# Graph kernel, sums of attention values: a table of PSUM addresses in place of VectorE additions

## The reference

```python
score = jnp.einsum('ehc,ehc->eh', q[dst], k[src]) / jnp.sqrt(OUT_C)
m = jax.ops.segment_max(score, dst, num_segments=n)
p = jnp.exp(score - m[dst])
denom = jax.ops.segment_sum(p, dst, num_segments=n)
alpha = p / jnp.maximum(denom[dst], 1e-16)
msg = v[src] * alpha[:, :, None]
out = jax.ops.segment_sum(msg, dst, num_segments=n)
```

## Time and profile before

| what | value |
|---|---|
| median of 3 runs | 6645.76 us (6632.06 to 6658.19) |
| profiled execution, first to last instruction | 6640.4 us |
| mean granted TensorE clock of the execution | 0.798 |
| PE, DVE, ACT, POOL busy | 69%, 58%, 33%, 40% |
| `clear_sums`, from the last instruction before to the first behind it | 3732.97 to 3741.61 us |
| `sum_values`, first to last instruction | 3741.6 to 4277.7 us |

### The profile page before, as it was taken

How to read it: one execution, slowest core, us unless ns; L and a number is a source line. 1 busy time by engine, 2 the same in 40 slices (tenths; PEclk the granted TensorE clock), 3 DMA queues, 4 the chain that set the end, 5 groups by cost and what they waited for, 6 DMA issues and landing times. The chain is left out here.

```text
span 6640.4 us, 100472 instructions
## 1 busy us (share of the span) xinstructions
PE 4599.9 (69%) x23624; PEld 3812.1 (57%) x23625; DVE 3837.8 (58%) x9293; ACT 2210.7 (33%) x4021; POOL 2644.9 (40%) x2513
## 2 busy tenths in 40 slices
PE   4455565565555455555555466549999999999997
PEld 2344444444322233333332355449999999999997
DVE  5466666666545566656566888864444466444443
ACT  0132223232212333333334133224444444334432
POOL 0355555555104565555550000014444444334432
PEclk7777777777787667666676676669999999999999
DMA  0333333333114455555552133233434344323332
GB/s 19 113 88 88 90 89 88 89 88 88 46 50 127 138 151 149 149 145 149 145 145 67 52 103 103 83 107 147 148 142 147 143 171 158 117 107 146 133 129 79
DMA packets 543144, 750.30 MB, mean 113 GB/s; under 512 B 57967, under 2 KB 441966, under 8 KB 542734
## 3 DMA queue, kind: packets, MB, share of 16 engines
q1 hardware_dynamic: 461182, 521.35, 23.4%
q0 software_dynamic: 81552, 224.63, 12.3%
HBM read 584.36 MB, written 161.41 MB: 112 GB/s over the span
## 5 line engine op out<-in xcount | busy, mean ns | idle before, releaser
L557 POOL DMA_INDIRECT arena<-table_kv,arena x1664 | 1684.5, 1012 | 1427.2 <-DVE arena L801 434.5
L2190 PE MATMUL ps<-moving,parts 128*128 128x384 f32 (+1 forms) x11662 | 2016.5, 331 | 38.2 <-ACT moving L2252 20.4
L2190 PEld LDWEIGHTS ps<-moving,parts 128*128 128x128 f32 x11662 | 1950.0, 188 | 71.9 <-ACT moving L2252 29.4
L2131 POOL CAST moving<-counts 128x1152 fp32r<-128x1152 uint8 (+1 forms) x420 | 476.7, 1135 | 1544.7 <-DVE counts L2265 935.6
L311 PE MATMUL ps<-by_place,by_lo 128*128 128x392 bf16 x1568 | 659.5, 525 | 438.7 <-issue 197.3
L320 ACT ACTIVATE counted<-ps 128x392 uint8<-128x392 f32 x1568 | 682.1, 506 | 619.7 <-PE ps L311 276.7
L2131 POOL CAST moving<-big 128x1152 fp32r<-128x1152 uint8 (+1 forms) x413 | 468.4, 1134 | 610.2 <-PE ps L2190 610.2
L667 PE MATMUL ps<-arena 128*128 128x137 f32 x1664 | 350.6, 372 | 370.1 <-DVE arena L801 358.5
L311 PEld LDWEIGHTS ps<-by_place,by_lo 128*128 128x128 bf16 x1568 | 190.0, 126 | 679.3 <-issue 433.9
L301 DVE TENSOR_TENSOR slots<-slots,counted 128x196 uint16 x1568 | 406.3, 259 | 289.0 <-issue 218.1
L667 PEld LDWEIGHTS ps<-arena 128*128 128x128 f32 x1664 | 301.2, 261 | 403.4 <-DVE big L764 190.0
(11 more groups left out here) (291 smaller groups left out, 5326.6 us busy)
## 6 DMA issues: line engine op xcount, KB each, us to landing
counts<-adjacency SPq DMA_DIRECT2D x53, 2352.0 KB, 8.5
big<-adjacency SPq DMA_DIRECT2D x52, 2352.0 KB, 8.6
adjacency<-slots SPq DMA_DIRECT2D x784, 98.0 KB
edge_values<-arena SPq DMA_DIRECT2D x208, 256.0 KB
arena<-edge_values SPq DMA_DIRECT2D x208, 256.0 KB, 3.1
arena<-table_kv,arena POOLq DMA_INDIRECT x1664
big<-table_norm SPq DMA_DIRECT2D x60, 192.0 KB, 5.7
big<-adjacency SPq DMA_DIRECT2D x7, 1568.0 KB, 6.5
```

The source lines that it names most:

```text
L557: pool.indirect_dma_start(m.ring4[r][:, k * 2 * D:(k + 1) * 2 * D], None, table, bass.IndirectOffsetOnAxis(m.src[:, j * HALF + k:j * HALF ...
L2131: pool.tensor_copy(to, of).then_inc(by_pool, 1)
L2190: mm = pe.matmul(m.bank(g % 2, n * P), d.parts[SOURCE[u]][:, s + q, t_, :], moving[:, q * n * P:(q + 1) * n * P], start=(s + q == 0 and t_ ...
```

## The change

The sums no longer pass through VectorE. The 49 blocks are 17 trios of three blocks; a trio's sums (3 x 132 = 396 columns) have one of the eight PSUM banks, trio number modulo 8, and all matmuls of a trio add up there. A half begins on TensorE with a register load of five places from a table, a matmul of zeros onto the bank whose trio is done (`closed`), then come the four matmuls at addresses from registers, then a wait until ScalarE has copied that bank to `m.sums` (`evacuated`), and a matmul of zeros with `start=True` that clears the bank. Each of the 208 halves, and 8 more behind them, moves one bank out, whether a trio is done or not; one that moves nothing of use writes behind the sums. ScalarE reads two of the places. GpSimd takes over the copy of the weights. Inputs of the matmuls have four buffers in place of two, the weighing and the comparison are one instruction each, and `clear_sums` is gone. The table is computed by VectorE in a chain of twenty instructions ahead of its copies in `softmax_rows`.

```diff
+def places_of_blocks(dve, m, ct, vec):
+    def then(op):
+        nonlocal count
+        count += 1
+        op.then_inc(vec, 1)
+        dve.wait_ge(vec, count)
...
+    then(dve.tensor_copy(block_f, m.block[0:1, :]))
+    then(dve.tensor_scalar(trio_i, m.block[0:1, :], 43.0, None, ALU.mult))
...
+    then(dve.tensor_tensor_scan(moved[:, 1:EVACS + 1], one, whole, 0.0, ALU.add, ALU.min))
...
+    then(dve.tensor_scalar(places[:, :, HALF], bank_i, 512.0, None, ALU.mult))
 def sum_values(nc, m, ct, edge_values):
...
+        @block.gpsimd
+        def _(pool):
+            def half(j, r):
+                wait(pool, used, j - 3)
+                pool.tensor_copy(msg[r][:, :, D:A1],
+                                 m.weight[:, ds(j * (HALF * H1), HALF * H1)].rearrange("p (k n) -> p k n", n=H1)).then_inc(weights_ready, 1)
...
         @block.tensor
         def _(pe):
+            regs = registers(nc, pe, "va1pe", HALF + 1)
+            def nought(at, opens):
+                return pe.matmul(m.ps[:, at], nothing[:, 0:P], nothing, start=opens, stop=not opens)
             def half(j, r):
-                pe.wait_ge(hit_ready, j + 1)
-                pe.wait_ge(weights_ready, j + 1)
-                pe.wait_ge(weighted, j + 1)
-                wait(pe, added, (j - 3) * HALF)
-                for k in range(HALF):
-                    mm = pe.matmul(summed(r, k), m.hit[:, r % 2, k, :], m.msg[:, r % 2, k, 0:A1], start=True, stop=True)
-                mm.then_inc(used, 1)
+                last = isinstance(j, int) and j >= 2 * TURNS
+                pe.load(regs, ct.tables[0:1, ds(j * PLACE, HALF + 1)])
+                done = ds(pe.snap(regs[HALF], min_val=0, max_val=(BANKS - 1) * 512), TRIO_SUMS)
+                nought(done, False).then_inc(closed, 1)
+                if not last:
+                    at = [pe.snap(x, min_val=0, max_val=most) for x in regs[:HALF]]
+                    pe.wait_ge(hit_ready, j + 1)
+                    pe.wait_ge(weights_ready, j + 1)
+                    pe.wait_ge(weighted, j + 1)
+                    for k in range(HALF):
+                        mm = pe.matmul(m.ps[:, ds(at[k], A1)], hit[r][:, k, :], msg[r][:, k, :], start=False, stop=False)
+                    mm.then_inc(used, 1)
+                pe.wait_ge(evacuated, j + 1)
+                nought(done, True)
...
         @block.scalar
         def _(act):
+            def convert(j, r):
                 act.wait_ge(hot, j + 1)
+                wait(act, used, j - 3)
+                act.activation(hit[r], hit16[:, r].rearrange("p n k -> p k n"), ACT.Copy).then_inc(hit_ready, 1)
+            def evacuate(j):
+                act.load(regs, ct.tables[0:1, ds(j * PLACE + HALF, 2)])
+                of = act.snap(regs[0], min_val=0, max_val=(BANKS - 1) * 512)
+                to = act.snap(regs[1], min_val=0, max_val=TRIOS * TRIO_SUMS)
+                act.wait_ge(closed, j + 1)
+                act.activation(m.sums[:, ds(to, TRIO_SUMS)], m.ps[:, ds(of, TRIO_SUMS)], ACT.Copy).then_inc(evacuated, 1)
...
+                    convert(4 * i + r + 1, (r + 1) % 4)
+                    evacuate(4 * i + r)
...
         @block.vector
         def _(dve):
+            def half(i, j, r):
+                one_hots(j + 1, (r + 1) % 4)
+                dve.wait_ge(read[r], 16 * i + 16)
+                weigh(j, r)
...
         softmax_weights(nc, m)
-        clear_sums(nc, m, BLOCKS * A1)
         sum_values(nc, m, ct, edge_values)
```

More of the change, by code:

```diff
@@ L48 @@
 SC = COLS * H1
+BANKS = 8
+TRIOS = -(-BLOCKS // 3)
+TRIO_SUMS = 3 * A1
+EVACS = 2 * TURNS + 8
+PLACE = 6
 F32 = mybir.dt.float32
@@ L988, in sum_values @@
 def sum_values(nc, m, ct, edge_values):
-    with Phase(nc, "va1", "used added made hot hit_ready weights_ready weighted read0 read1 read2 read3") as (
-            block, used, added, made, hot, hit_ready, weights_ready, weighted, read0, read1, read2, read3):
+    with Phase(nc, "va1", "used made hot hit_ready weights_ready weighted evacuated closed read0 read1 read2 read3") as (
+            block, used, made, hot, hit_ready, weights_ready, weighted, evacuated, closed, read0, read1, read2, read3):
@@ L994, in sum_values @@
         hit16 = m.stage_c[:, COLS // 2:COLS // 2 + 2 * HALF * P].bitcast(BF16).rearrange("p (a n k) -> p a n k", a=4, k=HALF)
+        nothing = m.prod[:, 0:TRIO_SUMS // 2].bitcast(BF16)
+        hit = [m.hit[:, 0], m.hit[:, 1], m.hitT[:, 0], m.hitT[:, 1]]
+        msg = [m.msg[:, 0, :, 0:A1], m.msg[:, 1, :, 0:A1]] + [
+            m.ring4[r][:, 0:HALF * A1].rearrange("p (k n) -> p k n", n=A1) for r in (4, 5)]
+        most = (BANKS - 1) * 512 + 2 * A1
         @block.sync
@@ L1007, in _ @@
                     load(4 * i + r, r)
-        summed = lambda r, k: m.bank(2 * r + k // 2)[:, 256 * (k % 2):256 * (k % 2) + A1]
+        @block.gpsimd
[4 more added lines that the diff above has]
+                                 m.weight[:, ds(j * (HALF * H1), HALF * H1)].rearrange("p (k n) -> p k n", n=H1)).then_inc(weights_ready, 1)
+            for j in range(4):
+                half(j, j)
+            with pool.Fori(1, TURNS // 2) as i:
+                for r in range(4):
+                    half(4 * i + r, r)
         @block.tensor
         def _(pe):
+            regs = registers(nc, pe, "va1pe", HALF + 1)
+            def nought(at, opens):
+                return pe.matmul(m.ps[:, at], nothing[:, 0:P], nothing, start=opens, stop=not opens)
             def half(j, r):
-                pe.wait_ge(hit_ready, j + 1)
-                pe.wait_ge(weights_ready, j + 1)
-                pe.wait_ge(weighted, j + 1)
-                wait(pe, added, (j - 3) * HALF)
-                for k in range(HALF):
-                    mm = pe.matmul(summed(r, k), m.hit[:, r % 2, k, :], m.msg[:, r % 2, k, 0:A1], start=True, stop=True)
-                mm.then_inc(used, 1)
+                last = isinstance(j, int) and j >= 2 * TURNS
[12 more added lines that the diff above has]
+                nought(done, True)
+            pe.wait_ge(made, 2)
+            for k in range(BANKS):
+                nought(slice(512 * k, 512 * k + TRIO_SUMS), True)
             for j in range(4):
@@ L1026, in _ @@
                     half(4 * i + r, r)
+            for j in range(2 * TURNS, EVACS):
+                half(j, None)
+            for k in range(BANKS):
+                nought(slice(512 * k, 512 * k + TRIO_SUMS), False)
         @block.scalar
         def _(act):
[L1030 to L1034, removed]
-                act.wait_ge(hot, j + 1)
-                act.activation(m.hit[:, r % 2], hit16[:, r].rearrange("p n k -> p k n"), ACT.Copy).then_inc(hit_ready, 1)
+            regs = registers(nc, act, "va1act", 2)
@@ L1038, in _ @@
+            convert(0, 0)
             for j in range(4):
-                half(j, j)
+                convert(j + 1, (j + 1) % 4)
+                evacuate(j)
             with act.Fori(1, TURNS // 2) as i:
                 for r in range(4):
-                    half(4 * i + r, r)
+                    convert(4 * i + r + 1, (r + 1) % 4)
+                    evacuate(4 * i + r)
+            for j in range(2 * TURNS, EVACS):
+                evacuate(j)
         @block.vector
         def _(dve):
-            sets = [registers(nc, dve, f"va1{k}") for k in range(2)]
@@ L1048, in blocks_of @@
[L1048 to L1077, removed]
-                dve.wait_ge(read[r], 16 * i + 16)
[L1079 to L1093, removed]
@@ new lines, in weigh, with one_hots @@
+            def weigh(j, r):
+                wait(dve, used, j - 3)
+                dve.tensor_tensor(
+                    msg[r][:, :, 0:D].rearrange("p k (n c) -> p k n c", c=C1),
+                    m.ring4[r].rearrange("p (k n) -> p k n", k=HALF)[:, :, 0:D].rearrange("p k (n c) -> p k n c", c=C1),
+                    copies(m.weight[:, ds(j * (HALF * H1), HALF * H1)].rearrange("p (k n) -> p k n", n=H1), 3, C1),
+                    ALU.mult).then_inc(weighted, 1)
+            def one_hots(j, r):
+                wait(dve, hit_ready, j - 3)
+                dve.tensor_tensor(hit16[:, r], ct.fours[:, 0:P, :], copies(local16[:, ds(j * HALF, HALF)], 1, P),
+                                  ALU.is_equal).then_inc(hot, 1)
@@ L1095, in _ @@
+            def half(i, j, r):
+                one_hots(j + 1, (r + 1) % 4)
+                dve.wait_ge(read[r], 16 * i + 16)
+                weigh(j, r)
+            dve.memset(nothing, 0.0).then_inc(made, 1)
             dve.tensor_copy(local16, m.local).then_inc(made, 1)
-            dve.wait_ge(made, 1)
-            one_hots(0, 0, slice(0, P // 2))
-            one_hots(0, 0, slice(P // 2, P))
+            dve.wait_ge(made, 2)
+            one_hots(0, 0)
             for j in range(4):
-                half(0, j, j, j < 2)
+                half(0, j, j)
@@ L1103, in _, with softmax_rows @@
                     half(i, 4 * i + r, r)
[L1104 to L1114, removed]
+def softmax_rows(nc, m, ct):
```

(5 more changed lines are left out.)

24 lines of the change are left out of this document (added).

## The result

The changed kernel takes 6598.6 us (median of four runs, 6590.4 to 6608.8), the kernel before 6648.6 in four runs of the same comparison: a ratio of 0.9936, interval 0.9922 to 0.9949. By the medians the gain is 50 us, by the ratio 43 (34 to 52), where 143.5 were forecast, and 6598.6 lies above the range. The profiled execution took 6590.4, the fastest of the four, with a span of 6588.5.

What follows compares the result with a forecast made beforehand. VectorE was taken to bound `sum_values`, afterwards a chain of 1.8 us in 216 halves: stage -140.7, `clear_sums` -7.3, table +4.5, together -143.5 us, giving 6502 us; range 6410 to 6590.

Steps and rivals of the forecast that it cites:

- address, load and places of the next half: TensorE's sequencer behind the wait for `evacuated`: 0.6 us plus 0.1 until the closing is issued; bounds 0 and 0.8.
- Closing to the start of the copy: From TensorE's closing matmul to the start of ScalarE's copy: 0.37 us, bounds 0.37 and 0.56.
- The copy: ScalarE's copy of 396 columns out of PSUM in each half: 0.50 us.
- TensorE seeing it: TensorE notices the finished copy and issues the opening matmul: 0.1 us, bounds 0.04 and 0.2.
- The branch: Loop branch of 0.21 us in every fourth half, with its register work: 0.1 us a half.
- The bound before (VectorE): In `sum_values` VectorE sets the pace; afterwards 1.1 us a half in place of 2.42, no longer the bound.
- The cover of GpSimd: GpSimd's copy of the weights takes under 0.83 us, has four halves of slack and costs nothing.
- `clear_sums`: Removing the clearing ahead of `sum_values`, 8.6 us with one stage boundary of about 1.3 staying: -7.3 us.
- The clock: TensorE in `sum_values` runs at 2.4 GHz but for the first few us, judged by its busy share in `softmax_rows`.
- a sequencer that reads on: Rival: TensorE's sequencer reads past the wait, hiding the load; 1.35 us a half, 6405 us; chance 0.17.
- The table: VectorE's twenty instructions in `softmax_rows`, some 14 us, 8.8 of it covered: +4.5 us, bounds 1 and 9.
- longer chain: Rival: more waits or register steps at each hand-over in `sum_values`; 2.2 us a half, 6589 us; chance 0.22.

Runs made afterwards that it cites:

- e2: Changed kernel with its table in three parts: four places loaded per half, banks and `m.sums` columns loaded once for four halves; 6499.4 us, 0.9783.
- e7: Changed kernel plus probe register loads of ten forms on ScalarE, their registers used by tiny copies; one word took 0.28 us, no kernel time given.
- e8: e6 with the wait for `weights_ready` moved from TensorE to VectorE; 6458.0 us, 0.9724, no difference from e6 that the runs can tell.
- e3: Changed kernel with the next half's register load issued ahead of the wait for `evacuated`, words unchanged; 6558.9 us, 0.9873.
- e5: Changed kernel plus probe register loads on TensorE and ScalarE ahead of `softmax_weights`, values unused; 6603.9 us in one run.
- e6: Changed kernel with both the split table of e2 and the early load of e3; 6460.1 us, 0.9718 of the kernel before.

## Why the prediction was wrong

**The failed step** is the term "address, load and places of the next half: 0.6 from 2609.8 to 2610.4, and 0.1 until the closing is issued. Five registers in place of four", with its upper bound of 0.8. It took the price of four registers for five: nothing more in the sum, and 0.1 in the bound. In the trace the term is 0.11 of address, 0.913 of load and 0.164 until the closing: 1.19 us in place of 0.7, above the bound. The row of 0.333 us was right, and e2 gets it back; but it was the row of a load of four words at a multiple of four, and the change loads five at a step of six. The diff showed the step of six, and no row of before had such a load. The trace of before had loads of four words and of one (L344), 0.333 and 0.302 us on TensorE, which made the count look free and said nothing of a fifth word or of an offset; that unknown should have had a bound of its own, well above one row of a better case.

The Trainium skill has a page that bears on it, "Runtime: NRT & Kernel Launch", Instruction fetch mechanics: a load costs about 200 ns for each register, said of loads out of HBM. The probes of e7 agree for single words (0.21 each from 0.28 to 0.91) and differ for four aligned ones (0.32 for all). Five registers by that page would be about 1.0 us, an estimate from its figure, against the 0.913 of the trace; it was not weighed in the prediction.

**The other terms of the chain.** Closing to the start of the copy: 0.475, within the bounds of 0.37 and 0.56; 0.37 was taken, because a wide row read in steps was set aside for a sum of a narrow row and columns (with 0.04 of hand-over, for which no row was given). What that sum left out is the register step that makes ScalarE's two addresses, which stands at the wait: it starts 0.37 behind the closing, just when the forecast had the copy start, takes 55 ns, and the copy starts 0.10 behind its start. The copy: 0.50, as forecast. TensorE seeing it: 0.05 in place of 0.1. The branch: 0.10, as forecast. Together 2.31 in place of 1.77: 0.49 from the load term, 0.10 from the hand-over, -0.05 from TensorE's seeing the copy. Times 216 the difference of 0.51 from the 1.8 taken is 110 us; the stage came out at 505.4 where 395.4 stood.

**What held.** The bound before (VectorE) and that it stops being one: the two instructions of a half take 0.70 and 0.41. The cover of GpSimd: its copy takes 0.20 us in the median, and taking TensorE's wait for it away changes nothing (e8). `clear_sums`: -7.5 for -7.3. The clock: 1.00 and 0.96 where 2.4 GHz was forecast, but the reason given does not carry it. It was that TensorE is busy the same share of time as in a window at 1.00; in the stage before it was busy 367.7 of 536.1 us, 69%, at 0.70, and in the stage after 361.5 of 522.0, also 69%, at 0.96. The level was right; that the share decides it is not shown.

**The sequencer at a wait.** The forecast gave 0.17 to a sequencer that reads on. It does not here: its next register step starts 0.05 us after the copy's end, and e3 shows that the wait is what holds it. That choice was right, and the 0.7 of the load term rightly stood in the chain. The Trainium skill says in "Advanced Engine Details and Errata", Sequencer Loop, that a waiting engine instruction sits in a queue while others are read; the trace disagrees with it for a register load behind the wait.

**The table** cost +0.8, where +4.5 stood with a lower bound of 1. Its chain in the changed kernel runs from its first row to the copy it delays:

```profile
3610.74 0.61 DVE L1011 CAST arena<-arena 1x896 f32<-1x896 int32 x1 [2.93 <-PEq L382]
3610.74 1.10 PE L1183 MATMUL ps<-ident,big 128*128 128x128 f32 x4 [4.72 <-PEq L382]
...
3611.39 0.61 DVE L1012 TENSOR_SCALAR arena<-arena 1x896 int32<-1x896 int32 x1
...
3621.18 0.69 DVE L1209 COPY big<-ps 128x512 f32<-128x512 f32 x1
...
3622.02 1.10 PE L1189 MATMUL ps<-arena 128*128 128x512 f32 x2 [1.80 <-DVE big L1209]
```

It takes 10.4 us in place of 14, so the copy starts 1.6 us later than before (10.4 against 8.8 behind the stage's start), not 5.4. From one instruction's end to the next it is 0.04 us (3611.35 to 3611.39), where 0.22 was taken from the earlier trace rows; that row of 0.22 is an instruction of 128 partitions that reads what the one before it wrote in the counting, and why it differs was not tried. One-input instructions of 896 columns are 0.61, not 0.8. TensorE waited 1.80 us once.

**The rival "longer chain"** (2.2 us, 6589) was nearest, 10 us off, for another reason than its own. It was built of small additions at each hand-over, and the range ended with it. The true cause was in the main one load at 2.7 times its price (0.913 for 0.333), and the range had no case for that.

## What to carry to other kernels

Where a register load stands behind a wait, it is part of the loop's pace like any instruction: give it its own row, by the number of words and by the offset that they start at. Four words at a multiple of four cost 0.32 to 0.33 us, five at an offset of two 1.13 to 1.24; so lay tables out in groups of four, pad where the count is odd, and issue the load ahead of the wait. And a price taken from a row holds for that row's form; if the diff shows another stride or count, its upper bound has to be that of the worst form.

## What was not expected of the hardware

- A load of three registers (0.70 us) takes more than twice as long as one of four (0.32), if the four start at a multiple of four words; four at another offset take 0.91.
- Loads cost a little more on TensorE's sequencer than on ScalarE's: one and the same word in the kernel before (L344, a flag) 0.302 against 0.278, four aligned words 0.33 against 0.32, and, from two tables, five words at an offset of two 1.24 against 1.13.
- None of the loads of e5, into registers that nobody reads, has a row in the trace; those of e7, with their registers used, all have.
- Two waits of TensorE in the source are one instruction in the trace (e6), and taking one of them out left the pace as it was (e8).
- TensorE's granted clock was 0.70 with TensorE busy 69% of the stage (before), 0.96 with 69% (after) and 0.98 with 91% (e6).
